# Position block 2 of a convolution in two fp32r parts, norm sums on ScalarE, skip weights in the block matrix

## The chip, the cores and the metric

The kernel runs on one core of a Trainium2 chip. The metric is the time of one execution on the device in microseconds, median of several runs. All 27 inputs lie in the chip's memory, and the output goes there.

## What is computed

Two layers, each of a mixing step and a feed-forward step, on x of 16 x 256 x 512 in fp32. The change is in the first mixing step, a long convolution:

```python
x = x + _L0_xattn_ref(_layernorm(x, axis=-1), L0_xattn_k, fside_S2_0, ctx_2048, ctx_2048, 8)

def _L0_xattn_ref(v, k, bias, x1, x2, num_heads):
    B, D, L = v.shape                        # 16, 256, 512
    H = D // num_heads                       # 32
    vr, x1r, x2r = (t.reshape(B, H, num_heads, L) for t in (v, x1, x2))
    kv = vr[:, :, :, None, :] * x2r[:, :, None, :, :]
    y = causal convolution of kv with k[h] along L
    skip = bias.reshape(H, num_heads)[None, :, :, None, None]
    y = y + kv * skip
    out = jnp.einsum('bhijl,bhil->bhjl', y, x1r)
    return out.reshape(B, D, L)
```

A layernorm follows at once (its rows feed the router of a mixture of eight experts), then that feed-forward step, an attention and a second feed-forward step. These are not touched.

## The kernel before, in words

Every engine has a queue of its own, in the order in which the Python code of a phase emits instructions (`p.do`, `p.dma`). Waits are semaphores: each `p.do` gets the tokens it waits for as its last arguments, and names its own result in the tables `T` and `U`. Nothing reorders the queues. An instruction that waits holds all that stands behind it on its engine.

The front phase (`front_phase`) does the convolution for 32 heads h. A head is 128 rows (16 batches x 8 channels) of 512 positions. The convolution is a Toeplitz product: positions are cut in four blocks of 128, and output block lb sums position blocks mb = 0 to lb, each a 128 x 128 matrix of filter values times a 128 x 512 matrix of products. The 512 columns are half of the (batch, i, j) triples, so each head is done in two halves, u = 0 and 1.

The steps of a head, with the lines of the code before:

- `load`: x, ctx in two layouts and the filter, by SyncE's queue, two heads ahead.
- `stats`, `shift`, `norm`: layernorm of the input rows. `stats` calls `layernorm_stats` (L115): bn_stats (L117), bn_aggr (L118) and an addition (L119) on VectorE, then a power of -1/2 on GpSimd (L120). `shift` (L315) is one product on VectorE, `norm` (L319) one ScalarE operation, which gives xn.
- `weigh` (L324) on VectorE: w = xn * skip * ctx. `skips`: a fp32 matmul of w with the block matrix ones_b (L338), and a product with ctx (L340), which gives sk. `residual` (L345) on GpSimd adds x.
- `filt`, `filt_lo`: the Toeplitz matrices. TensorE reverses them into PSUM tile PT (L301, L309), and ScalarE copies the high part th (L302) and the low part tl (L310). PT is one tile, so L309 waits for L302. `t0` (L311) on GpSimd is th + tl, in fp32.
- `turn`: TensorE transposes xn into PSUM tile PV (L331), ScalarE copies it (vt, L333).
- `product` (L354), GpSimd: kf, the products of a position block, five steps ahead of its use.
- `parts`, `lows`: kh (L361, ScalarE) is kf rounded to fp32r, kl (L369) the rest, on VectorE for block 0 and on GpSimd for block 1. Blocks 2 and 3 have no parts.
- `conv`: matmuls into PSUM tiles Y0 to Y3. Position blocks 0 and 1 take three fp32r matmuls (L386: th kh, tl kh, th kl), blocks 2 and 3 one fp32 matmul each (L381: t0 kf), which the trace shows as two records. VectorE multiplies Y with ctx (z, L393) and reduces over i (R, L399).
- `finish` (L404, L406) for the head before: R is transposed back, and out2 (VectorE) adds sk to it. That is x after the step. `stats0`, `shift0` (L475), `norm0` (L479), `turn0` (L486, L488) and `logit` (L493, L495) are its layernorm and the router's logits; `best` (L504, L505) picks two experts. turn, turn0 and logit share the PSUM tile PV.

The main loop writes all this out for u = 0 and 1 and lb = 0 to 3, eight steps per head. What stands in a step decides the queues' order. Of the loop's placement rules, these matter here:

```python
                if u == 1 and lb == 2 and h + 2 < n_heads:
                    stats(h + 2)
                if u == 0 and lb == 3 and more:
                    turn(h + 1)
                n = (2 * h + u) * 4 + lb + 4
                if n + 1 < len(units):
                    product(*units[n + 1])
                if n < len(units):
                    parts(*units[n], low=False)
                conv(h, u, lb, units[n] if n < len(units) and lb == 0 else None)
                if u == 0 and lb == 3 and h:
                    finish(h - 1)
                if h and u == 1:
                    (stats0, shift0, norm0, turn0)[lb](h - 1)
```

In the first eight heads, a shared weight of the next step is also split in the step u = 0, lb = 1 (L463 on ScalarE, L464 on GpSimd).

Of the kernel before, what the change touches and what calls it, by code (L numbers as in the profile page):

```python
# [123 lines left out]
def front_phase(nc, ctx, d, before, xa, idx, gat, n_heads=NHC):  # L124
# [88 lines left out]
    pad = m.sb("pad", [128, 3688])  # L213
# [187 lines left out]
    def finish(h):  # L401
# [4 lines left out]
        T["out2", h] = U["PR",] = p.do("vector", lambda e: e.tensor_tensor(xt[:, h % 4, :], sk[:, s, :], PR[:, :], ALU.add), g("pr", h), g("sk", h))  # L406
# [293 lines left out]
    load(1)  # L700
    stats(0)
# [17 lines left out]
    for h in range(n_heads):  # L719
        more = h + 1 < n_heads  # L720
        for u in range(2):
            for lb in range(4):
                if u == 0 and lb == 2 and h + 2 < n_heads:
                    load(h + 2)
                    clear(3)
                if u == 1 and lb == 2 and h + 2 < n_heads:
                    stats(h + 2)
# [17 lines left out]
                conv(h, u, lb, units[n] if n < len(units) and lb == 0 else None)  # L745
# [1008 lines left out]
```

How the kernel before makes its waits and increments, by code:

```python
    def emit(self, e, eng):  # L69
        seen = {}
        def wait(sem, v):
            if seen.get(id(sem), 0) < v:
                eng.wait_ge(sem, v)
                seen[id(sem)] = v
        for sem, v in self.before:
            wait(sem, v)
        for fn, waits, inc in self.q[e]:
            for w in waits:
                if w is not None:
                    wait(*w)
            ins = fn(eng)
            if inc:
                ins.then_inc(*inc)
# [1647 lines left out]
                def run(eng, e=e):  # L1733
                    for p in phases:
                        p.emit(e, eng)
                    if e == "sync":
                        for sem, v in before:
                            eng.wait_ge(sem, v)
```

## Time and profile before

| | before |
|---|---|
| median of 3 runs | 3311.36 us (3310.96 to 3315.59) |
| profiled execution, its own time | 3308.17 us |
| its span | 3306.4 us |
| TensorE busy (matmuls) | 3190.9 us, 97% |
| VectorE busy | 2164.9 us, 65% |
| ScalarE busy | 1269.4 us, 38% |
| GpSimd busy | 1014.3 us, 31% |
| L354, kf on GpSimd | 256 of 1179 ns |
| L393 and L399, z and reduce on VectorE | 256 each, of 680 and 684 ns |

The profile is of one execution. Times in it are microseconds from the start of the span. PE is TensorE, PEld its weight loads, DVE VectorE, ACT ScalarE, POOL GpSimd, SP SyncE. L393 is line 393 of the kernel. The ends of matmuls are modelled, so what a matmul costs is read from where the next one starts. The convolution ends at about 640 us, and TensorE shows as busy in nearly all of it. The shares of the whole span say little of it, since the last four fifths are other stages.

### The profile page before, as it was taken

How to read it: one execution, taken by the hardware profiler on the slowest of the kernel's cores; microseconds unless marked ns; L12 is line 12 of the kernel's file. 1: busy time of each engine (PE TensorE's matmuls, PEld its weight loads, DVE VectorE, ACT ScalarE, POOL GpSimd, SP SyncE). 2: the span in 40 equal slices, each digit the busy share in tenths (PEclk: the TensorE clock that was granted, in tenths of full speed). 3: DMA queues.
4: the chain of work that ended last, by engine and by line, in shares of the span. 5: the costliest groups of instructions: out<-in, count | busy, mean ns of one | idle time of the engine just before them, and what ended most of it. 6: DMA issues, size and time to landing. Idle time of an engine off the chain costs nothing.

```text
span 3306.4 us, 51716 instructions
## 1 busy us (share of the span) xinstructions
PE 3190.9 (97%) x18613; PEld 2698.1 (82%) x18613; DVE 2164.9 (65%) x5818; ACT 1269.4 (38%) x3059; POOL 1014.3 (31%) x1085
## 2 busy tenths in 40 slices
PE   7999999999999699999999999999997999999999
PEld 4666666688899579999999999999996777777777
DVE  6888888756555477888777778878876433322232
ACT  2333333233444255555555555555554311111111
POOL 6877777535111222222222222222201000000000
PEclk9999999999999899999999999999998999999999
DMA  4544443269544421111111111111101200000000
GB/s 131 156 139 131 135 136 90 79 201 311 180 153 153 177 93 53 46 46 46 46 46 46 46 46 46 46 46 44 34 14 55 81 26 26 26 26 26 26 13 13
DMA packets 123664, 267.21 MB, mean 81 GB/s; under 512 B 17668, under 2 KB 18316, under 8 KB 123414
## 3 DMA queue, kind: packets, MB, share of 16 engines
q1 hardware_dynamic: 100022, 186.40, 17.9%
q0 software_dynamic: 23392, 77.51, 7.1%
q8 instruction: 153, 2.51, 0.3%
q14 instruction: 97, 0.79, 0.1%
HBM read 159.29 MB, written 104.56 MB: 80 GB/s over the span
## 4 chain that ended last, share of the span: by engine, by line
PE 79%; DVE 10%; POOL 7%; ACT 1%; DMA 1%; issue 1%; SPq 0%; POOLq 0%; DVEq 0%; ACTq 0%
PE g_PH L1051 11%; PE g_O L1079 11%; PE t_U L1515 10%; PE t_S L1467 9%; PE t_PO L1502 5%; PE t_M L1451 5%; POOL c_kf L354 3%; PE t_T L1489 3%; PE f_Y L916 3%; PE f_Y L687 2%; PE f_Y L386 2%; PE t_M L1406 2%; PE f_Y L381 2%; DVE c_R L399 2%; DVE c_z L393 2%; PE t_M L1388 2%
## 5 line engine op out<-in xcount | busy, mean ns | idle before, releaser
L1477 ACT ACTIVATE t_pr<-t_sm,t_nb 128x256 f32<-128x256 f32 x512 | 256.5, 502 | 368.8 <-DVE t_nb L1473 368.8
L1064 DVE CAST g_hh<-g_hf 128x512 fp32r<-128x512 f32 x128 | 55.0, 429 | 481.8 <-PE g_O L1079 476.8
L1421 POOL TENSOR_TENSOR t_r<-t_r 128x256 f32<-128x256 f32 x128 | 96.0, 750 | 773.6 <-DVE t_rw L1483 457.6
L354 POOL TENSOR_TENSOR c_kf<-c_vt,c_ct 128x512 f32<-128x512 f32 x256 | 296.7, 1179 | 0.2 <-PE f_Y L381 0.2
L1063 ACT ACTIVATE g_hf<-g_PH,g_b1s 128x512 f32<-128x512 f32 x128 | 88.2, 689 | 536.9 <-PE g_PH L1051 536.9
L1484 DVE TENSOR_SCALAR t_pr<-t_pr,t_rw 128x256 f32<-128x256 f32 x512 | 223.5, 436 | 18.2
L386 PE MATMUL f_Y<-c_kh,c_th 128*128 128x512 f32 x448 | 200.9, 448 | 9.3 <-ACT c_kh L361 9.3
L1051 PE MATMUL g_PH<-g_xh,g_w1h 128*128 128x512 f32 x512 | 205.5, 401 | 1.5 <-DVE g_xl L1039 1.5
L1079 PE MATMUL g_O<-g_w2h,g_hh 128*128 128x512 f32 x512 | 205.2, 401 | 0.0
L1051 PE MATMUL g_PH<-g_xh,g_w1l 128*128 128x512 f32 x512 | 203.0, 397 | 0.0
L1051 PE MATMUL g_PH<-g_xl,g_w1h 128*128 128x512 f32 x512 | 203.0, 396 | 0.0
L1515 PE MATMUL t_U<-t_vol,t_oth 128*128 128x512 f32 x512 | 202.3, 395 | 0.0
L1515 PE MATMUL t_U<-t_voh,t_otl 128*128 128x512 f32 x512 | 202.0, 395 | 0.0
L1079 PE MATMUL g_O<-g_w2l,g_hh 128*128 128x512 f32 x512 | 201.7, 394 | 0.0
L1079 PE MATMUL g_O<-g_w2h,g_hl 128*128 128x512 f32 x512 | 201.5, 394 | 0.0
L1515 PE MATMUL t_U<-t_voh,t_oth 128*128 128x512 f32 x512 | 200.9, 392 | 0.0
L1473 DVE CUSTOM_DVE_ANT_0 t_sm<-t_S,t_mk 128x256 f32<-128x256 f32 x512 | 194.8, 418 | 7.7 <-PE t_S L1467 7.7
L393 DVE TENSOR_TENSOR c_z<-f_Y,c_ct 128x512 f32<-128x512 f32 x256 | 174.1, 680 | 35.7 <-PE f_Y L381 35.5
L1494 DVE TENSOR_TENSOR t_ptl<-t_T,t_pth 128x512 fp32r<-128x512 f32 x256 | 175.6, 686 | 15.5 <-ACT t_pth L1493 15.4
L381 PE MATMUL f_Y<-c_kf,c_t 128*128 128x512 f32 x384 | 185.4, 591 | 0.0
L399 DVE TENSOR_REDUCE c_R<-c_z 128x64 f32<-128x512 f32 x256 | 175.0, 684 | 6.7
L386 PE MATMUL f_Y<-c_kh,c_tl 128*128 128x512 f32 x448 | 178.1, 397 | 0.0
(361 smaller groups left out, 9666.5 us busy)
## 6 DMA issues: line engine op xcount, KB each, us to landing
xs<-c_zero SPq DMA_DIRECT2D x71, 256.0 KB, 5.2
f_xg<-xs SPq DMA_DIRECT2D x71, 256.0 KB, 2.8
ys<-f_yt POOLq DMA_DIRECT2D x71, 256.0 KB, 2.4
c_tr<-kpad SPq DMA_DIRECT2D x60, 256.0 KB, 4.6
f_xg<-xn SPq DMA_DIRECT2D x40, 256.0 KB, 4.4
c_xt<-x SPq DMA_DIRECT2D x32, 256.0 KB, 3.5
c_cr<-ctx SPq DMA_DIRECT2D x32, 256.0 KB, 3.8
c_ct<-ctxh SPq DMA_DIRECT2D x32, 256.0 KB, 4.3
```

Source lines behind the costliest of these rows:

```text
L354: T["kv", h] = T["kv1", n] = p.do("gpsimd", lambda e: e.tensor_tensor(o, iv, ic, ALU.mult), g("vt", h), g("ct", h), g("kl", n - 8), g("kh" ...
L381: last = p.do("tensor", lambda e, c=c, mb=mb: e.matmul(Y[y % 4][:, :], t0[:, s, c], kf[:, v, mb, :], start=False, stop=mb == lb), g("t0", ...
L386: last = p.do("tensor", lambda e, a=a, b_=b_, c=c, mb=mb, i=i: e.matmul(Y[y % 4][:, :], a[:, s, c], b_[:, v, mb, :], start=(mb == 0 and i ...
L393: T["z", h] = T["z1", y] = p.do("vector", lambda e: e.tensor_tensor(zz.rearrange("p (b j i) -> p b j i", i=8, j=8), iv, ic, ALU.mult), las ...
L399: T["red", y] = T["R", h] = p.do("vector", lambda e: e.tensor_reduce(rr, zr, AXX, ALU.add), g("z1", y), g("pr", h - 2))
L1051: T["ph", n] = p.do("tensor", lambda e, kk=kk, a=a, b_=b_, i=i: e.matmul(ph[:, :], a[:, k, kk, :], b_[:, s, kk, :], start=i == 0, stop=i = ...
L1079: tk = p.do("tensor", lambda e, a=a, b_=b_, t=t, fin=fin, c=c, beg=beg: e.matmul(O[t][:, :], a[:, n % 2, c], b_[:, k, :], start=beg, stop= ...
L1467: a = p.do("tensor", lambda e, t=t, j=j, q=q, k=k: e.matmul(PS1[:, 256 * t:256 * t + 256], q, k[:, s, :], start=j == 0, stop=j == 4), g("q ...
L1473: T["am", N] = am = p.do("vector", lambda e, t=t, k4=k4: e.tensor_tensor_reduce(out=sm[:, k4, :], in0=PS1[:, 256 * t:256 * t + 256], in1=m ...
L1477: T["ex", x] = p.do("scalar", lambda e, t=t, k4=k4: e.activation(pr[:, N % 2, t, :], sm[:, k4, :], ACT.Exp, bias=nb[:, k4, 0:1], scale=-1. ...
L1484: T["nm", x] = p.do("vector", lambda e, t=t, k4=k4: e.tensor_scalar(pr[:, N % 2, t, :], pr[:, N % 2, t, :], rw[:, k4, 1:2], None, ALU.mult ...
L1515: a = p.do("tensor", lambda e, t=t, tt=tt, j=j, o=o, w=w: e.matmul(PU[t][:, :], o[:, N % 3, tt], w[:, h, :], start=h == 0 and j == 0, stop ...
```

## The change

Three things are changed, all in the front phase.

Position block 2 is split in two fp32r parts as blocks 0 and 1 were: kh on ScalarE, kl on GpSimd for a half with u = 1 and on VectorE for one with u = 0. Its products are three fp32r matmuls in place of a fp32 one. Only block 3, which only meets filter block 0, stays fp32, so t0 shrinks to 128 columns.

The variances of both layernorms no longer come from bn_stats. For the input's norm, ScalarE sums the row (`total`), VectorE makes the negative mean, ScalarE sums the squares of the differences (`squares`). For the second norm, out2 becomes a tensor_tensor_reduce that also sums, then `squares0`. VectorE divides and adds epsilon, GpSimd takes the power as before. The shifts become products of two tiles.

The skip weight moves from w into the matrix of the skip product: ScalarE writes bs, ones_b times skip, per head, and w is a plain product.

```diff
-    kh = m.sb("kh", [128, 2, 2, 512], F32R)
-    kl = m.sb("kl", [128, 2, 2, 512], F32R)
-    t0 = m.sb("t0", [128, 2, 256])
+    kh = m.sb("kh", [128, 2, 3, 512], F32R)
+    kl = m.sb("kl", [128, 2, 3, 512], F32R)
+    t0 = m.sb("t0", [128, 2, 128])
...
+    def total(h):
+        s = h % 2
+        S_ = su[:, 0, s, :]
+        a = p.do("scalar", lambda e: e.activation(ju[:, :], xt[:, h % 4, :], ACT.Copy, accum_out=S_[:, 0:1]), g("x", h), g("xn", h - 2), U.get("ju"))
+        U["ju"] = a
+        T["mean", h] = p.do("vector", lambda e: e.tensor_scalar(S_[:, 1:2], S_[:, 0:1], -1.0 / 512.0, None, ALU.mult), a, g("xn", h - 2))
+
+    def squares(h):
...
+        T["sq", h] = U["ju"] = p.do("scalar", lambda e: e.activation(ju[:, :], xt[:, h % 4, :], ACT.Square, bias=S_[:, 1:2], accum_out=S_[:, 2:3]),
+                                    T["mean", h], g("x", h), U["ju"])
...
     def stats(h):
         s = h % 2
-        T["rs", h] = layernorm_stats(p, xt[:, h % 4, :], st[:, s, :], ag[:, s, :], rs[:, s, :], mhalf, g("x", h), g("xn", h - 2), c_mh)
+        S_ = su[:, 0, s, :]
+        a = p.do("vector", lambda e: e.tensor_scalar(S_[:, 3:4], S_[:, 2:3], 1.0 / 512.0, EPS, ALU.mult, ALU.add), T["sq", h], g("rs", h - 2))
+        T["rs", h] = p.do("gpsimd", lambda e: e.tensor_tensor(rs[:, s, :], S_[:, 3:4], mhalf, ALU.pow), a, c_mh, g("xn", h - 2))
...
     def shift(h):
         s = h % 2
-        T["nm", h] = p.do("vector", lambda e: e.tensor_scalar(nm[:, s, :], ag[:, s, 0:1], rs[:, s, :], -1.0, ALU.mult, ALU.mult), g("rs", h), g("xn", h - 2))
+        T["nm", h] = p.do("vector", lambda e: e.tensor_tensor(nm[:, s, :], su[:, 0, s, 1:2], rs[:, s, :], ALU.mult), g("rs", h), T["mean", h], g("xn", h - 2))
...
     def weigh(h):
         s = h % 2
-        T["w", h] = p.do("vector", lambda e: e.scalar_tensor_tensor(out=w[:, s, :], in0=xn[:, s, :], scalar=skip[:, h:h + 1],
-                                                                   in1=cr[:, s, :], op0=ALU.mult, op1=ALU.mult),
-                         g("xn", h), c_sk, g("cr", h), g("psk", h - 2))
+        T["bs", h] = p.do("scalar", lambda e: e.activation(bs[:, s, :], ones_b, ACT.Copy, scale=skip[:, h:h + 1]), c_ob, c_sk, g("psk", h - 2))
+        T["w", h] = p.do("vector", lambda e: e.tensor_tensor(w[:, s, :], xn[:, s, :], cr[:, s, :], ALU.mult), g("xn", h), g("cr", h), g("psk", h - 2))
...
-        if mb > 1:
+        if mb > 2:
             return
         T["kh", n] = p.do("scalar", lambda e: e.activation(kh[:, v, mb, :], kf[:, v, mb, :], ACT.Copy), g("kv1", n), g("mmu", 2 * h + u - 2))
-        if low or mb % 2:
+        if low or mb == 1 or mb == 2 and u:
             lows(h, u, mb)
...
-        eng = "gpsimd" if mb % 2 else "vector"
+        eng = "gpsimd" if mb == 1 or mb == 2 and u else "vector"
...
-        T["out2", h] = U["PR",] = p.do("vector", lambda e: e.tensor_tensor(xt[:, h % 4, :], sk[:, s, :], PR[:, :], ALU.add), g("pr", h), g("sk", h))
+        S_ = su[:, 1, s, :]
+        T["out2", h] = U["PR",] = p.do("vector", lambda e: e.tensor_tensor_reduce(
+            out=xt[:, h % 4, :], in0=PR[:, :], in1=sk[:, s, :], scale=1.0, scalar=0.0, op0=ALU.add, op1=ALU.add, accum_out=S_[:, 0:1]),
+            g("pr", h), g("sk", h), gu("xb", h - 2))
+        U["mean", h] = p.do("vector", lambda e: e.tensor_scalar(S_[:, 1:2], S_[:, 0:1], -1.0 / 512.0, None, ALU.mult), T["out2", h], gu("xb", h - 2))
+        squares0(h)
...
+                if u == 1 and lb == 0 and h + 2 < n_heads:
+                    total(h + 2)
+                if u == 1 and lb == 1 and h + 2 < n_heads:
+                    squares(h + 2)
                 if u == 1 and lb == 2 and h + 2 < n_heads:
                     stats(h + 2)
...
-                conv(h, u, lb, units[n] if n < len(units) and lb == 0 else None)
+                conv(h, u, lb, units[n] if n < len(units) and (lb == 0 or lb == 2 and not units[n][1]) else None)
```

`squares0`, `stats0` and `shift0` have the same form on the second half of su. In the new code the lines are: mean L423 and L295, squares0 L490, total L293, squares L300, the variances L496 (second norm) and L306 (input's norm), the shifts L501 and L329, kl L382, w L339, bs L338, turn's copy L346.

VectorE's queue, from out2 (head h - 1) to the input's variance of head h + 2. Before:

```order
L406 TENSOR_TENSOR c_xt<-c_sk,f_PR 128x512
L504 MAX c_mx<-c_lg 128x8
L505 MAX_INDEX c_ix<-c_mx,c_lg 128x8
L393 TENSOR_TENSOR c_z<-f_Y0,c_ct 128x512
L369 TENSOR_TENSOR c_kl<-c_kf,c_kh 128x512
L399 TENSOR_REDUCE c_R<-c_z 128x64
L117 BN_STATS c_st0<-c_xt 128x6
L118 BN_AGGR c_ag0<-c_st0 128x2
L119 TENSOR_SCALAR c_rs0<-c_ag0 128x1
```

Now:

```order
L420 ISA c_xt,c_su<-f_PR,c_sk 128x512
L420 ISA c_su 128x1
L423 TENSOR_SCALAR c_su<-c_su 128x1
L530 MAX c_mx<-c_lg 128x8
L531 MAX_INDEX c_ix<-c_mx,c_lg 128x8
L295 TENSOR_SCALAR c_su<-c_su 128x1
L406 TENSOR_TENSOR c_z<-f_Y0,c_ct 128x512
L382 TENSOR_TENSOR c_kl<-c_kf,c_kh 128x512
L412 TENSOR_REDUCE c_R<-c_z 128x64
L496 TENSOR_SCALAR c_su<-c_su 128x1
```

The mean of head h + 2 (L295), which needs ScalarE's `total`, stands ahead of z of block 0.

ScalarE's queue in the same place, from turn's copy vt to the second norm's xb. Before:

```order
L333 ACTIVATE c_vt<-f_PV 128x512
L302 ACTIVATE c_th<-f_PT 128x512
L361 ACTIVATE c_kh<-c_kf 128x512 x2
L310 ACTIVATE c_tl<-f_PT 128x512
L479 ACTIVATE c_xb<-c_xt,c_nm0,c_rs0 128x512
```

Now:

```order
L346 ACTIVATE c_vt<-f_PV 128x512
L490 ACTIVATE c_ju,c_su<-c_xt,c_su 128x512
L293 ACTIVATE c_ju,c_su<-c_xt 128x512
L316 ACTIVATE c_th<-f_PT 128x512
L374 ACTIVATE c_kh<-c_kf 128x512
L300 ACTIVATE c_ju,c_su<-c_xt,c_su 128x512
L374 ACTIVATE c_kh<-c_kf 128x512
L324 ACTIVATE c_tl<-f_PT 128x512
L374 ACTIVATE c_kh<-c_kf 128x512
L505 ACTIVATE c_xb<-c_xt,c_nm0,c_rs0 128x512
```

Squares of head h - 1 and total of head h + 2 stand ahead of th, squares of h + 2 between the kh of blocks 0 and 1, and the new kh of block 2 ahead of xb.

GpSimd's queue, a head in the later part (the products of three blocks in a row are one row with x3). Now:

```order
L367 TENSOR_TENSOR c_kf<-c_vt,c_ct 128x512 x3
L382 TENSOR_TENSOR c_kl<-c_kf,c_kh 128x512
L367 TENSOR_TENSOR c_kf<-c_vt,c_ct 128x512
L382 TENSOR_TENSOR c_kl<-c_kf,c_kh 128x512
L367 TENSOR_TENSOR c_kf<-c_vt,c_ct 128x512 x2
L497 TENSOR_TENSOR c_rs<-c_su,f_mhalf 128x1
L367 TENSOR_TENSOR c_kf<-c_vt,c_ct 128x512
L382 TENSOR_TENSOR c_kl<-c_kf,c_kh 128x512
L307 TENSOR_TENSOR c_rs<-c_su,f_mhalf 128x1
L325 TENSOR_TENSOR c_t<-c_th,c_tl 128x128
L367 TENSOR_TENSOR c_kf<-c_vt,c_ct 128x512
L358 TENSOR_TENSOR c_sk<-c_sk,c_xt 128x512
```

The second kl is new, the rest stands as before: the first power, kf, kl, the second power, t0, kf, sk.

## Rows read from the trace of the kernel before

**Rows 1.** Engines in one head: us, busy us and instructions, PE, PEld, DVE, ACT, POOL
```profile
284.50:303.50 19.00, 18.73 (x80) 12.97 (x79) 16.67 (x33) 6.28 (x11) 14.72 (x15) 1.00 0.46 139
```
**Rows 2.** Chain of waits through one head: start us, us, what
```profile
282.49 0.63 PE f_PV L331 x4
...
286.28 0.70 DVE c_z L393
...
287.69 0.59 DVE c_xt L406
...
288.64 0.59 DVE c_z L393
...
290.42 0.61 DVE c_st L117
...
291.27 0.15 DVE c_rs L119
...
298.06 2.51 POOL c_kf L354 x2
...
300.60 0.63 ACT c_kh L361
...
301.44 0.63 PE f_PV L331 x4
```
**Rows 3.** The same chain in two of the first eight heads, same instruction
```profile
123.29 2.51 POOL c_kf L354 x2
...
142.74 2.51 POOL c_kf L354 x2
```
**Rows 4.** Waits from 60 to 560 us: us in total, times, longest
```profile
PE f_PV L331 <- ACT c_lg L495: 13.2, 26, 1.2
```
**Rows 5.** Timeline of TensorE, convolution: start us, us, what
```profile
302.61 0.40 PE L386 MATMUL f_Y<-c_kh,c_th 128*128 128x512 f32 x1
302.85 0.40 PE L386 MATMUL f_Y<-c_kh,c_tl 128*128 128x512 f32 x1
...
303.32 1.88 PE L381 MATMUL f_Y<-c_kf,c_t 128*128 128x512 f32 x4
...
305.03 0.60 PE L404 MATMUL f_PR<-f_ident,c_R 128*128 128x128 f32 x4
```
**Rows 6.** ScalarE elsewhere: sums in the attention (timeline), a bias in a feed-forward (groups)
```profile
1603.70 0.51 ACT L1477 ACTIVATE t_pr<-t_sm,t_nb 128x256 f32<-128x256 f32 x1 [1.66 <-DVE t_nb L1473]
1604.12 0.19 ACT L1477 ACTIVATION_READ_ACCUMULATOR t_pr<-t_sm,t_nb 128x1 f32 x1
...
L1063 ACT ACTIVATE g_hf<-g_PH,g_b1s 128x512 f32<-128x512 f32 x128 | 88.2, 689 | 536.9 <-PE g_PH L1051 536.9
```
**Rows 7.** Timeline of VectorE in the attention: a tensor_tensor_reduce and its read-out
```profile
1603.25 0.41 DVE L1473 CUSTOM_DVE_ANT_0 t_sm<-t_S,t_mk 128x256 f32<-128x256 f32 x1
1603.59 0.07 DVE L1473 DVE_READ_ACCUMULATOR2_ANT t_nb<- 128x1 f32 x1
```
**Rows 8.** Timeline of GpSimd in the same head
```profile
291.50 0.55 POOL L120 TENSOR_TENSOR c_rs<-c_rs,f_mhalf 128x1 f32<-128x1 f32 x1 [4.06 <-DVE c_rs L119]
292.02 1.07 POOL L354 TENSOR_TENSOR c_kf<-c_vt,c_ct 128x512 f32<-128x512 f32 x1
293.04 1.28 POOL L369 TENSOR_TENSOR c_kl<-c_kf,c_kh 128x512 fp32r<-128x512 f32 x1
294.54 0.55 POOL L120 TENSOR_TENSOR c_rs<-c_rs,f_mhalf 128x1 f32<-128x1 f32 x1 [0.22 <-DVE c_rs L119]
295.06 0.73 POOL L311 TENSOR_TENSOR c_t<-c_th,c_tl 128x256 f32<-128x256 f32 x1
```
**Rows 9.** The instruction w (L324) and the kf beside it; min/median/max ns of w
```profile
L324 DVE SCALAR_TENSOR_TENSOR c_w<-c_xn,c_skip,c_cr x32: 750/1342/1462, 13.3 to 604.8; 128x512 f32<-128x512 f32 x32
...
297.27 1.34 DVE L324 SCALAR_TENSOR_TENSOR c_w<-c_xn,c_skip,c_cr 128x512 f32<-128x512 f32 x1
...
298.02 1.52 POOL L354 TENSOR_TENSOR c_kf<-c_vt,c_ct 128x512 f32<-128x512 f32 x1
```

More of the change, by code:

```diff
@@ L175, in front_phase @@
     w = m.sb("w", [128, 2, 512])
+    bs = m.sb("bs", [128, 2, 128])
     vt = m.sb("vt", [128, 2, 4, 128])
     kf = m.sb("kf", [128, 2, 4, 512])
-    kh = m.sb("kh", [128, 2, 2, 512], F32R)
-    kl = m.sb("kl", [128, 2, 2, 512], F32R)
-    t0 = m.sb("t0", [128, 2, 256])
+    kh = m.sb("kh", [128, 2, 3, 512], F32R)
+    kl = m.sb("kl", [128, 2, 3, 512], F32R)
+    t0 = m.sb("t0", [128, 2, 128])
     z = m.sb("z", [128, 3, 512])
@@ L185, in front_phase @@
     xb = m.sb("xb", [128, 2, 512])
+    ju = m.sb("ju", [128, 512])
+    su = m.sb("su", [128, 2, 2, 4])
     xT = m.sb("xT", [128, 4, 128])
-    st0 = m.sb("st0", [128, 2, 6])
-    ag0 = m.sb("ag0", [128, 2, 2])
     rs0 = m.sb("rs0", [128, 2, 1])
@@ L212, in front_phase @@
     rb = m.sb("rb", [8, 256])[:, :]
-    pad = m.sb("pad", [128, 3688])
+    pad = m.sb("pad", [128, 1168])
     sw = m.sb("sw", [128, 8192], F32R)
@@ L289, in split_filters @@
         T["kp",] = p.dma("gpsimd", ko, lambda e: e.dma_start(d["kpad"].rearrange("q h x -> h q x"), f32(kq[:, :, :])), a, b_)
+    def total(h):
[5 more added lines that the diff above has]
+    def squares(h):
+        s = h % 2
+        S_ = su[:, 0, s, :]
+        T["sq", h] = U["ju"] = p.do("scalar", lambda e: e.activation(ju[:, :], xt[:, h % 4, :], ACT.Square, bias=S_[:, 1:2], accum_out=S_[:, 2:3]),
+                                    T["mean", h], g("x", h), U["ju"])
     def stats(h):
         s = h % 2
-        T["rs", h] = layernorm_stats(p, xt[:, h % 4, :], st[:, s, :], ag[:, s, :], rs[:, s, :], mhalf, g("x", h), g("xn", h - 2), c_mh)
+        S_ = su[:, 0, s, :]
+        a = p.do("vector", lambda e: e.tensor_scalar(S_[:, 3:4], S_[:, 2:3], 1.0 / 512.0, EPS, ALU.mult, ALU.add), T["sq", h], g("rs", h - 2))
+        T["rs", h] = p.do("gpsimd", lambda e: e.tensor_tensor(rs[:, s, :], S_[:, 3:4], mhalf, ALU.pow), a, c_mh, g("xn", h - 2))
     def filt(h):
@@ L310, in filt_lo @@
             T["tl", h] = p.do("scalar", lambda e: e.activation(tl[:, s, :], PT[:, :], ACT.Copy), g("pt", h), g("mm", h - 2))
-        T["t0", h] = p.do("gpsimd", lambda e: e.tensor_tensor(t0[:, s, :], f32(th[:, s, 0:256]), f32(tl[:, s, 0:256]), ALU.add), g("th", h), g("tl", h), g("mm", h - 2))
+        T["t0", h] = p.do("gpsimd", lambda e: e.tensor_tensor(t0[:, s, :], f32(th[:, s, 0:128]), f32(tl[:, s, 0:128]), ALU.add), g("th", h), g("tl", h), g("mm", h - 2))
     def shift(h):
         s = h % 2
-        T["nm", h] = p.do("vector", lambda e: e.tensor_scalar(nm[:, s, :], ag[:, s, 0:1], rs[:, s, :], -1.0, ALU.mult, ALU.mult), g("rs", h), g("xn", h - 2))
+        T["nm", h] = p.do("vector", lambda e: e.tensor_tensor(nm[:, s, :], su[:, 0, s, 1:2], rs[:, s, :], ALU.mult), g("rs", h), T["mean", h], g("xn", h - 2))
     def norm(h):
@@ L337, in skips @@
         s = h % 2
-        T["psk", h] = p.do("tensor", lambda e: e.matmul(PSK[:, :], ones_b, w[:, s, :], start=True, stop=True),
-                           c_ob, g("w", h), g("sx", h - 1))
+        T["psk", h] = p.do("tensor", lambda e: e.matmul(PSK[:, :], bs[:, s, :], w[:, s, :], start=True, stop=True),
+                           g("bs", h), g("w", h), g("sx", h - 1))
         a = p.do("vector", lambda e: e.tensor_tensor(sk[:, s, :], cr[:, s, :], PSK[:, :], ALU.mult), g("psk", h), g("out2", h - 2))
@@ L379, in conv @@
             c = slice(128 * (lb - mb), 128 * (lb - mb) + 128)
-            if mb > 1:
+            if mb > 2:
                 last = p.do("tensor", lambda e, c=c, mb=mb: e.matmul(Y[y % 4][:, :], t0[:, s, c], kf[:, v, mb, :], start=False, stop=mb == lb),
@@ L467, in shared_weights, with squares0 @@
             ahead.append((fetch(part[0]), *part[1:]))
+    def squares0(i):
+        s = i % 2
+        S_ = su[:, 1, s, :]
+        U["sq", i] = U["ju"] = p.do("scalar", lambda e: e.activation(ju[:, :], xt[:, i % 4, :], ACT.Square, bias=S_[:, 1:2], accum_out=S_[:, 2:3]),
+                                    U["mean", i], T["out2", i], U["ju"])
     def stats0(i):
         s = i % 2
-        U["rs", i] = layernorm_stats(p, xt[:, i % 4, :], st0[:, s, :], ag0[:, s, :], rs0[:, s, :], mhalf, T["out2", i], gu("xb", i - 2), c_mh)
+        S_ = su[:, 1, s, :]
+        a = p.do("vector", lambda e: e.tensor_scalar(S_[:, 3:4], S_[:, 2:3], 1.0 / 512.0, EPS, ALU.mult, ALU.add), U["sq", i], gu("rs", i - 2))
+        U["rs", i] = p.do("gpsimd", lambda e: e.tensor_tensor(rs0[:, s, :], S_[:, 3:4], mhalf, ALU.pow), a, gu("xb", i - 2), c_mh)
     def shift0(i):
         s = i % 2
-        U["nm", i] = p.do("vector", lambda e: e.tensor_scalar(nm0[:, s, :], ag0[:, s, 0:1], rs0[:, s, :], -1.0, ALU.mult, ALU.mult), U["rs", i], gu("xb", i - 2))
+        U["nm", i] = p.do("vector", lambda e: e.tensor_tensor(nm0[:, s, :], su[:, 1, s, 1:2], rs0[:, s, :], ALU.mult), U["rs", i], U["mean", i], gu("xb", i - 2))
     def norm0(i):
@@ L700, in front_phase @@
     load(1)
+    total(0)
+    squares(0)
     stats(0)
@@ L709, in front_phase @@
     residual(0)
+    total(1)
+    squares(1)
     stats(1)
```

2 lines of the change are left out of this document (removed).

## The prediction

> **What bounds the kernel now.** I read the whole-span page first (the front phase, with the convolution, is the first fifth of the span), then the stretch of one head, then the chain of waits through it, then the timelines of each engine. One head of the convolution takes 18.95 us: in that stretch TensorE is busy 18.7 us of 19.0, VectorE 16.7, GpSimd 14.7, ScalarE 6.3 [rows 1]. That looks like a TensorE bound, but the chain [rows 2] is not one of matmuls. It is a ring that closes once per head. TensorE turns xn (L331), runs block 3 of the convolution and hands over after 3.79 us (282.49 to 286.28). VectorE works through its list for 8.26 us (286.28 to 294.54), up to the variance that GpSimd's power waits for. GpSimd then runs its own list for 6.06 us (294.54 to 300.60), and ScalarE makes kh, copies the logits out of PV and lets TensorE turn the next head after 0.84 us. 3.79 + 8.26 + 6.06 + 0.84 = 18.95. TensorE waits only 13.2 us in 26 heads for that last step, 0.5 us a head [rows 4]; so its own work is 18.45 us a head. The first eight heads have a ring of 19.45 us [rows 3], since ScalarE splits a shared weight in it.
>
> So the ring, not an engine's busy time, has to be recalculated. I take t = 0 where VectorE starts z of block 3 (u = 0).
>
> **TensorE.** A fp32r matmul of 512 columns starts 0.24 us after the one before (302.61, 302.85), a fp32 one takes 0.855 us (two from 303.32 to 305.03) [rows 5]; three parts cost 0.70. A half head (u) has three fp32 products, of which the two with position block 2 are split (in output blocks 2 and 3): four times 0.155 a head, 0.62 us off 18.45, leaves 17.8 us. One of the four lies in the ring: 3.79 becomes 3.64.
>
> **VectorE up to the first variance.** Before: z, reduce and out2 end at t = 2.00 (287.69 + 0.59), z of block 0 starts at 2.36, z, kl and reduce take 1.78, and the BN pair is done so that L119 stands at 4.99 (291.27) [rows 2]. Now: out2 also sums. The nearest rows are the attention's tensor_tensor_reduce with PSUM as one source, 0.41 us for 256 columns with a start-to-start of 0.34 [rows 7], and half of out2's 0.68; so the sum costs the read-out of some 0.08 alone. The mean (L423) takes 0.15 and hand-overs 0.08: t = 2.31. Now ScalarE must square (L490) and then total the head after next (L293), in this order, and **VectorE's L295 stands ahead of z of block 0 and waits for both**. A bare 512-column copy takes 0.63 (L361 in [rows 2]), one with a bias 0.69 [rows 6]; the read-out of the accumulator starts 0.42 after a 0.51 instruction and takes 0.19 [rows 6], so adds 0.10. Each also waits for the other's end through ju. Squares: 0.75 + 0.11; total: 0.63 + 0.11 + 0.03. ScalarE is done at 3.94 and z of block 0 starts at 4.05, 1.7 us later than before. ScalarE goes on with th (next start 0.54 later) and kh, which is done at 5.08: kl starts at 5.12, not 4.65. Reduce, then L496: 6.32, done 6.47. Removing bn_stats and bn_aggr (0.83 us, 290.42 to 291.27 less hand-over) is in this already: it gains 0.83, and the waits cost 1.7 + 0.5. GpSimd's first power starts at t = 6.54, where it started at 5.22 (291.50).
>
> **GpSimd.** Power 0.52, kf 1.02, kl 1.25, start to start [rows 8], must end before the second power: 6.54 + 2.79 = 9.33, where before it was free at 8.0 and waited for VectorE until 8.26. Then power, t0, kf, sk and two kf, 6.06 in all before. t0 has 128 columns for 256: 0.73 against kl's 1.28 for 512 gives 0.28 less.
>
> **The port.** w runs 0.75 us at the start, while GpSimd idles, and 1.34 in the median [rows 9]. One w starts at 297.27, beside sk, which ends where the kf behind it starts, at 298.02; w ends at 298.61, and that kf takes 1.52 for the usual 1.07 [rows 8, 9]. So sk finishes first, then w runs 0.6, and kf stands still for most of that. So, as I read it, a VectorE instruction with two tensors in SBUF and a GpSimd one exclude each other. By the Trainium skill (SBUF — State Buffer, Who interferes with whom) this is a lock held for a whole instruction, and a VectorE operation with two SBUF inputs takes part in it. The trace agrees, by 1.52 against 1.07 us. Another page speaks otherwise of w: the Trainium skill (Vector Engine (DVE) Microarchitecture Reference, Points that are easy to get wrong) has a scalar_tensor_tensor with two fp32 SBUF sources run at half rate; by it w would end some 0.6 us earlier, the kf in the ring might lose its 0.45 us of standing still, and the sum would be 13 us lower. The 0.75 us of the undisturbed w speaks against it; no run so far has the other form in its place.
>
> What this makes of the change: w as a plain product saves 0.07 at most (0.75 to 0.68) and still collides, so I count nothing; its copies of the weights (L338, a 128-column ScalarE operation of some 0.3 us) hide in ScalarE's idle time. No DMA is added or moved on any queue; the store of out2 starts 0.08 us later. The new kl of block 2 on VectorE (u = 0 of the next head) falls to t = 10.1, when GpSimd is in power and t0: it runs 0.60 between two GpSimd instructions and pushes t0 back by that, 0.60 in the ring. The shifts nm (L501, L329) are now products of two SBUF tensors of one column. Such a small one is not in the trace beside a busy GpSimd; bounds are nothing and the rest of the kl it meets. L501 comes up at t = 8.31, kl ends at 9.33: with the lock L306 ends at 9.61 and the second power starts at 9.68, without it at 9.35. I take the first, since the form is what the lock went by in [rows 9]. The other new kl (u = 1, GpSimd, 1.28 us) stands where GpSimd now idles 4.1 us before the first power [rows 8], so costs nothing, also with the 1.28 us that the shared weights add in eight heads; if the cover went, it would add 1.28. kh of block 2 hides in ScalarE, except where it stands between.
>
> **Sum.** 3.64 + 9.68 + (6.06 - 0.28 + 0.60 = 6.38) + 0.84 = 20.54 us with all port effects; 3.64 + 9.35 + 5.78 + 0.84 = 19.61 with none of the new ones. I take 20.4, nearer the first, +1.45 us a head. Twenty-nine heads (1 to 29) have both powers and a next turn: +42 us. The prologue gains 0.5 (ScalarE sums head 1 before it splits the filters), the first and last heads give back about 1 (their matmuls, 0.62 each). The profiled execution took 3308.2 us (span 3306.4), so its like would take about 3350; the median of the runs is 3311.4, 3.2 above, and goes to **3353**. A measurement of this kernel tells 0.2% (6.6 us) from no change.
>
> A second ring would hold the kernel even if GpSimd's were short. filt_lo on TensorE needs PT, which th frees. th now stands behind squares and total, and ends at t = 3.94 + 0.6; TensorE would reach filt_lo at t = 3.4 and from there has 10.85 us of work to the next turn. 3.64 + 4.54 + 10.85 = 19.0. So the matmul time saved in block 2 is lost here at the least.
>
> **Rivals.**
> - *TensorE becomes the bound, faster.* If ScalarE's two sums were there when VectorE has picked the best (0.36 us after the mean), the list to the second power would lose its two BN groups (0.83 each) and gain three small ones: some 7.1 us, and the ring 3.64 + 7.3 + 5.8 (6.4) + 0.84 = 17.6 to 18.2. Then TensorE's 17.8 decides: about 1.05 x 30 = 32 us less, 3279. For it: VectorE's busy time does fall. Against it: ScalarE starts only after out2 and the two sums take 1.6 us. It decides only if the wait at L295 is under 0.2 us; I have 1.3. 11%, with all weaker gains.
> - *The ring through PT alone, no change.* GpSimd gets ahead, and 19.0 us stands against 18.95: 3312. It needs the first power about 1.3 us earlier than I have it. 7%.
> - *No new port effect.* 19.6 to 20.0 us a head: 0.65 to 1.05 x 29 gives 3330 to 3342. For it: one-column operations may not take part. 13%.
> - *Accumulating costs full extra passes.* If out2's sum took 1.34, as w looks, +0.66 more a head, 21.1 us: 3374. Against it the 0.41 of rows 7. 7%.
> - *The forecast*, 20.1 to 20.8 us, 3344 to 3366: 62%.
>
> **How the numbers follow.** The range from 3322 to 3368 holds the forecast and the third rival, and leaves out the first, most of the second, and the fourth; about 8 in 10. Slower by over 0.2%: 62 + 13 + 7 = 82%; within: 7%; faster: 11%.
>
> **What would show it.** Right: a period of 20.4 us between turns; VectorE idle over 1 us ahead of z of block 0, put down to ScalarE's sum; the first power over 1 us later after z of block 3; TensorE waiting for c_lg by more than 1 us a head and for th at filt_lo; GpSimd without a gap between its kl and the second power; nm at 1 us where it was 0.2. Wrong, if the period is under 19 us, or if TensorE waits nowhere: then ScalarE's sums are shorter than a copy plus a read-out, or VectorE has enough else to do. That the fp32r parts are not cheaper would show as a block 2 over 2.2 us from its first matmul to its last start.

## The result and the profile after

The changed kernel takes 3343.16 us (median of 4 runs, 3342.24 to 3344.13); the kernel before, beside it on the same chip, takes 3311.16 us. The ratio is 1.0097 with a 95% interval from 1.0084 to 1.0109: 32 us slower, where 42 us were forecast. The profiled execution took 3342.2 us, its span 3340.5.

The chain of waits through one head, the same stretch as in [rows 2] (columns: start us, us, what):

```profile
295.48 0.63 PE f_PV L344 x4
...
299.09 0.70 DVE c_z L406
...
300.50 0.60 DVE c_xt L420
...
301.33 0.82 ACT c_ju L490 x2
...
302.24 0.72 ACT c_ju L293 x2
...
303.34 0.63 ACT c_kh L374
...
304.00 0.69 DVE c_kl L382
...
307.17 1.11 DVE c_nm L501
...
308.43 0.55 POOL c_rs L307
308.98 0.88 POOL c_t L325
...
314.67 0.63 ACT c_kh L374
...
315.51 0.63 PE f_PV L344 x4
```

It is still a ring of one head, now of 315.51 - 295.48 = 20.03 us, 1.08 more than before. Its pieces are TensorE's 3.61 (295.48 to 299.09), VectorE's 9.34 (to the second power at 308.43), GpSimd's 6.24 (to 314.67) and the turn's 0.84. New in it are two pairs of ScalarE, the squares and the total, between out2 and kl: each is a sum and its read-out. The same chain in two of the early heads:

```profile
110.31 0.63 PE f_PV L344 x4
...
130.85 0.63 PE f_PV L344 x4
```

These are 20.54 us apart, for 19.45 in [rows 3]. Twenty-nine heads by 1.08 are 31.3 us. The last reduction of the convolution starts at 672.2 us (L412), where it started at 642.5 (L399): 29.7 us later, which fits the ring less the 1.5 us that the prediction has the first and last heads give back. The two spans are 34.1 us apart; the 4 us behind the convolution, in stages that weren't touched, are not explained by any run.

VectorE's timeline around its two waits (start us, us, engine, line, operation, out<-in, shapes, in brackets the idle time before it and what ended it):

```profile
302.99 0.15 DVE L295 TENSOR_SCALAR c_su<-c_su 128x1 f32<-128x1 f32 x1 [1.35 <-ACT c_ju L293]
...
304.00 0.69 DVE L382 TENSOR_TENSOR c_kl<-c_kf,c_kh 128x512 fp32r<-128x512 f32 x1 [0.26 <-ACT c_kh L374]
...
307.17 1.11 DVE L501 TENSOR_TENSOR c_nm<-c_su,c_rs 128x1 f32<-128x1 f32 x1
308.21 0.14 DVE L306 TENSOR_SCALAR c_su<-c_su 128x1 f32<-128x1 f32 x1
...
308.87 0.68 DVE L382 TENSOR_TENSOR c_kl<-c_kf,c_kh 128x512 fp32r<-128x512 f32 x1
...
310.06 0.84 DVE L329 TENSOR_TENSOR c_nm<-c_su,c_rs 128x1 f32<-128x1 f32 x1
```

GpSimd's timeline over the same time:

```profile
305.43 0.55 POOL L497 TENSOR_TENSOR c_rs<-c_su,f_mhalf 128x1 f32<-128x1 f32 x1 [3.78 <-DVE c_su L496]
...
306.97 1.30 POOL L382 TENSOR_TENSOR c_kl<-c_kf,c_kh 128x512 fp32r<-128x512 f32 x1
308.43 0.55 POOL L307 TENSOR_TENSOR c_rs<-c_su,f_mhalf 128x1 f32<-128x1 f32 x1 [0.16 <-DVE c_su L306]
308.94 0.91 POOL L325 TENSOR_TENSOR c_t<-c_th,c_tl 128x128 f32<-128x128 f32 x1
```

VectorE stands idle for 1.35 us at L295, where it waits for ScalarE's total. Its shift of one column (L501) takes 1.11 us: it starts at 307.17 and ends at 308.28, as GpSimd's kl does (306.97 + 1.30 = 308.27). The second variance (L306) is queued behind it, and GpSimd's second power waits for that (0.16 us). Then the new kl of block 2 on VectorE (308.87) and GpSimd's t0 meet; t0 has half the columns it had and takes 0.91 us, where the whole one took 0.73 [rows 8] and the half one takes 0.46 in e4 below, with no kl beside it.

ScalarE's timeline shows the two sums, each an instruction and its read-out:

```profile
301.33 0.72 ACT L490 ACTIVATE c_ju<-c_xt,c_su 128x512 f32<-128x512 f32 x1 [4.10 <-DVE c_su L423]
301.96 0.19 ACT L490 ACTIVATION_READ_ACCUMULATOR c_ju<-c_xt,c_su 128x1 f32 x1
302.24 0.63 ACT L293 ACTIVATE c_ju<-c_xt 128x512 f32<-128x512 f32 x1
302.77 0.19 ACT L293 ACTIVATION_READ_ACCUMULATOR c_ju<-c_xt 128x1 f32 x1
```

The waits from 60 to 560 us, as in [rows 4] (us in total, times, longest):

```profile
PE f_PT L323 <- ACT c_th L316: 20.4, 24, 0.9
PE f_PV L344 <- ACT c_lg L521: 17.9, 23, 1.2
PE f_PV L512 <- ACT c_xb L505: 11.5, 25, 2.3
```

TensorE waits 0.85 us a head for th, 0.78 for the turn and 0.46 for xb, 2.1 in all, so that its own work is 17.9 us. The fp32r parts save about what they should (0.55 of 18.45, where 0.62 was forecast); TensorE waits for three things now instead of one, and the saving goes into these waits.

### The profile page after: what moved, and what is told of

It is laid out like the page before. It is cut to its first block, busy times and chain, and to the rows that moved or that the text cites. A ratio compares the mean times of both kernels' runs of the same rounds, so it can differ in the third digit from the quotient of the medians.

```text
span 3340.5 us, 52458 instructions
## 1 busy us (share of the span) xinstructions
PE 3182.0 (95%) x18741; PEld 2717.8 (81%) x18741; DVE 2185.8 (65%) x5818; ACT 1382.3 (41%) x3347; POOL 1060.8 (32%) x1117
## 4 chain that ended last, share of the span: by engine, by line
PE 78%; DVE 9%; POOL 7%; ACT 4%; issue 2%; DMA 1%; SPq 0%; POOLq 0%; ACTq 0%; DVEq 0%
PE g_PH L1085 11%; PE g_O L1113 11%; PE t_U L1549 10%; PE t_S L1501 9%; PE t_PO L1536 5%; PE t_M L1485 4%; POOL c_kf L367 3%; PE t_T L1523 3%; PE f_Y L950 3%; PE f_Y L713 2%; PE f_Y L399 2%; PE t_M L1440 2%; DVE c_R L412 2%; PE f_PSK L925 2%; PE t_M L1422 2%
## 5 line engine op out<-in xcount | busy, mean ns | idle before, releaser
L399 PE MATMUL f_Y<-c_kh,c_th 128*128 128x512 f32 x576 | 236.6, 411 | 9.2 <-ACT c_kh L374 9.2
L399 PE MATMUL f_Y<-c_kl,c_th 128*128 128x512 f32 x576 | 228.1, 396 | 0.0
L399 PE MATMUL f_Y<-c_kh,c_tl 128*128 128x512 f32 x576 | 227.4, 395 | 0.0
L1527 ACT ACTIVATE t_pth<-t_T 128x512 fp32r<-128x512 f32 x256 | 151.6, 592 | 67.2 <-PE t_T L1523 66.3
```

The costliest lines, as they stand in the source:

```text
L399: last = p.do("tensor", lambda e, a=a, b_=b_, c=c, mb=mb, i=i: e.matmul(Y[y % 4][:, :], a[:, s, c], b_[:, v, mb, :], start=(mb == 0 and i ...
```

## The experiments

In every one the time was taken in five rounds beside the kernel before. The kernel before took 3310.61 us beside the first four experiments, 3310.44 beside the next four (e5 to e8, on another chip) and 3308.59 beside the last three.

### One part of the change at a time

**e1_split: the split of block 2 alone.** To the kernel before is added only this part of the change, here its two main places:

```
-        if mb > 1:
+        if mb > 2:
             return
...
-        if low or mb % 2:
+        if low or mb == 1 or mb == 2 and u:
             lows(h, u, mb)
...
```

with t0 on 128 columns, and BN statistics and w as they were.

> The kernel before with the split of position block 2 alone (bn_stats and w as before). By the ring: TensorE's step 3.79 to 3.64, t0 0.28 shorter, and the new kl on VectorE falls between the second power and t0 and holds t0 back by 0.5 to 0.6; 18.95 becomes 19.0 us a head, so 3311 to 3318 us. Rival: TensorE's time decides, 0.62 us less a head, 3292 us. A kl that did not exclude GpSimd's work would give 18.5 us a head, 3297 us.

3315.52 us (3313.53 to 3324.64), ratio 1.0019 (1.0009 to 1.0029). The profiled execution is the slowest of the nine, and its span is 16.5 us longer; but its last reduction of the convolution starts only 5.8 us later than before (648.3 for 642.5 us). The rest lies behind the convolution, in stages that the split doesn't touch. In the later heads the ring is 18.97 us, nearly as before, but from other pieces: TensorE 3.62, VectorE 8.27, GpSimd 6.24, 0.84. What TensorE wins in the ring, t0 loses against VectorE's kl; its chain shows it (start us, us, what):

```profile
319.64 0.55 POOL c_rs L120
320.19 0.89 POOL c_t L311
```

In the early heads, though, no turn of TensorE is in the chain; it runs from GpSimd to VectorE and back, with the shared weight's residual (L464, 1.30 us at 133.39), a kf, the new kl (L369) and the kf that VectorE's next kl needs, in a row:

```profile
124.51 0.55 POOL c_rs L120
...
135.71 1.25 POOL c_kl L369
...
144.29 0.55 POOL c_rs L120
```

That ring is 144.29 - 124.51 = 19.78 us, 0.33 over the 19.45 of before [rows 3]: there the new kl on GpSimd has lost its cover.

**e2_skip: the skip weights alone.**

```
-        T["w", h] = p.do("vector", lambda e: e.scalar_tensor_tensor(... scalar=skip[:, h:h + 1], ...
+        T["bs", h] = p.do("scalar", lambda e: e.activation(bs[:, s, :], ones_b, ACT.Copy, scale=skip[:, h:h + 1]), ...
+        T["w", h] = p.do("vector", lambda e: e.tensor_tensor(w[:, s, :], xn[:, s, :], cr[:, s, :], ALU.mult), ...
```

> The kernel before with the skip weights in the block matrix alone; w is a plain product. By the reading that w takes 0.7 us in either form and the rest is waiting for GpSimd: w's median stays over 1.2 us, the ring stays at 18.9 to 19.0, 3311 us (3308 to 3313). Rival (the old form runs at half rate): w takes 0.7, kf is not held back, 18.5 us a head, 3298 us.

3309.94 us, ratio 0.9999 (0.999 to 1.0008): nothing, and the ring stays at 18.95. All w of this kernel, min/median/max ns:

```profile
L326 DVE TENSOR_TENSOR c_w<-c_xn,c_cr x32: 691/1346/1469, 13.8 to 604.8; 128x512 f32<-128x512 f32 x32
```

The plain product takes 1346 ns in the median, the form before took 1342 [rows 9]. Only the undisturbed one differs, 691 against 750 ns. The form of the instruction was never what made w long; GpSimd beside it is.

**e3_stats: the norm statistics alone**, all of the change but the other two parts.

> The changed kernel with blocks and skip weights as before, so only the norm statistics are changed. By the ring: VectorE's step is 9.34 as in the changed kernel, the others 3.79, 6.06 and 0.84: 20.0 us a head, 3343 us (3338 to 3348). Rival (the loss comes from the new kl and the copies of the split): under 3320 us.

3340.75 us (3337.37 to 3342.9), ratio 1.009 (1.0075 to 1.0106), 30 of the 32 us, with a ring of 19.99 us (294.75 to 314.74 in its chain). The shift of the second norm is as long as in the changed kernel. The other one is not (VectorE, then GpSimd, as in the timelines above):

```profile
306.60 1.09 DVE L501 TENSOR_TENSOR c_nm<-c_su,c_rs 128x1 f32<-128x1 f32 x1
...
308.99 0.15 DVE L328 TENSOR_TENSOR c_nm<-c_su,c_rs 128x1 f32<-128x1 f32 x1
```

```profile
308.36 0.72 POOL L324 TENSOR_TENSOR c_t<-c_th,c_tl 128x256 f32<-128x256 f32 x1
309.04 1.07 POOL L367 TENSOR_TENSOR c_kf<-c_vt,c_ct 128x512 f32<-128x512 f32 x1
```

It comes up at 308.99, as t0 ends (308.36 + 0.72) and 0.05 us ahead of the next kf, and takes 0.15 us; as I read it, it gets in between the two. In the changed kernel the same shift (L329, 310.06 to 310.90) comes up beside a kf (309.82 to 310.88) and ends with it, though sk follows on GpSimd at once (310.85). So such an instruction waits for the one GpSimd instruction that runs, not for GpSimd to be idle.

### One wait of the change at a time

**e4_ptr: the changed kernel with the two shifts in another form.** The same product, with the inverse deviation as the operand that holds one value per partition:

```
-... e.tensor_tensor(nm0[:, s, :], su[:, 1, s, 1:2], rs0[:, s, :], ALU.mult)
+... e.tensor_scalar(nm0[:, s, :], su[:, 1, s, 1:2], rs0[:, s, :], None, ALU.mult)
```

> The changed kernel with both shifts nm as tensor_scalar with a pointer operand, the form of before (one SBUF tensor as input in place of two). If the two-tensor form waits for GpSimd: nm takes 0.2 us in both places, the second power starts 0.1 to 0.2 us earlier (where kl ends), the period is 19.8 to 19.9, 3337 to 3340 us. If nm is long for another cause: nm stays at 1.1 and 0.84 us, 3343 us.

3334.6 us (3332.33 to 3336.03), ratio 1.0075 (1.0061 to 1.0088), 8.5 us under the changed kernel and a little better than expected; the shifts take about 0.2 us again. The ring is 19.80 us. It lost 0.23 and not the 0.9 by which L501 is shorter, because the second power has to wait for GpSimd's own kl in any case. It follows that kl at once now, where it stood 0.16 us behind it. VectorE's kl of block 2 comes up earlier too and holds back this power (0.95 us for 0.55) instead of t0, which takes 0.43 for 0.88; the two together take 1.38 us for 1.43. Chain of waits:

```profile
324.26 1.26 POOL c_kl L382
325.51 0.95 POOL c_rs L307
326.47 0.43 POOL c_t L325
```

**e5_early: the changed kernel with the total a step earlier**, so that its result is there when VectorE comes to L295:

```
-                if u == 1 and lb == 0 and h + 2 < n_heads:
+                if u == 0 and lb == 3 and h + 2 < n_heads:
                     total(h + 2)
```

> The changed kernel with the sum of head h + 2 (total and its mean) one step earlier, so that it no longer stands behind squares0 and ahead of th. By the ring: VectorE no longer waits at the mean; th and kh of block 0 end 0.76 us earlier, kl, reduce and the first power follow, 20.03 becomes 19.3 us a head, 3319 us (3316 to 3323). Rival (the wait at the mean is slack, kl or GpSimd decides): 3338 us or more.

3320.76 us (3316.68 to 3323.74), ratio 1.0031 (1.0019 to 1.0042), 22 us under the changed kernel, as expected. VectorE does L295 ahead of z of block 3 now, and only the squares, th and kh stand between out2 and kl:

```profile
289.59 0.14 DVE L295 TENSOR_SCALAR c_su<-c_su 128x1 f32<-128x1 f32 x1
...
294.46 0.69 DVE L382 TENSOR_TENSOR c_kl<-c_kf,c_kh 128x512 fp32r<-128x512 f32 x1 [0.94 <-ACT c_kh L374]
```

kl stands 4.09 us after z of block 3 (290.37), for 4.91 in the changed kernel; the ring is 19.21 us (the second powers start at 298.88 and 318.09). One statement in another place, with no operation changed, gives back two thirds of the loss.

**e6_early_ptr: both edits.**

> The one before and the shifts nm as tensor_scalar with a pointer, together. If the two add (0.76 and 0.23 a head): 19.0 to 19.1 us, 3311 to 3314 us, about the time of the kernel before. If TensorE's queue takes over through th and filt_lo: the same as the sum of head h + 2 alone, 3319 us.

3313.97 us (3308.35 to 3316.03), ratio 1.0007 (0.9998 to 1.0016), ring 19.00 us (313.95 to 294.95, second power). The two add up: 22 and 7 us. With them the change costs nothing measurable, but gains nothing either. It is still the same ring: TensorE's 3.61, VectorE's 5.52 from z of block 3 to the first power, GpSimd's 9.03 from there on, now without a wait for the second variance, and the turn's 0.84. VectorE still waits for kh in it, which stands behind the squares and th:

```profile
309.68 0.69 DVE L382 TENSOR_TENSOR c_kl<-c_kf,c_kh 128x512 fp32r<-128x512 f32 x1 [0.94 <-ACT c_kh L374]
```

### Another order, and a gain

In the ring GpSimd's second power can't start until VectorE has come to the input's variance, late in its list. Both powers could be asked for together, at the point of the first.

**e7_order: the kernel before, with both variances and powers behind kl of block 1.**

```
-                if u == 1 and lb == 2 and h + 2 < n_heads:
-                    stats(h + 2)
...
+                if u == 1 and lb == 1:
+                    if h:
+                        stats0(h - 1)
+                    if h + 2 < n_heads:
+                        stats(h + 2)
...
-                if h and u == 1:
+                if h and u == 1 and lb:
                     (stats0, shift0, norm0, turn0)[lb](h - 1)
```

> The kernel before with its arithmetic unchanged and only the order changed: both variances and powers stand together in the step u = 1, lb = 1, behind the kl of block 1 on GpSimd. By the ring: the second power starts 2.1 us earlier, the ring falls to about 16.8 us, and TensorE's own 18.45 us decide: 3296 us (3292 to 3300), TensorE without a wait at the turn. Rival (TensorE's matmuls already bound the kernel before, ring or not): 3308 to 3311 us.

3322.28 us (3317.05 to 3325.96), ratio 1.0035 (1.0024 to 1.0046), where 3296 was expected: a miss. The chain no longer passes GpSimd at all:

```profile
346.34 0.70 DVE c_z L393
...
349.29 1.26 DVE c_kl L369
...
355.07 0.14 DVE c_nm L475
...
355.23 0.82 ACT c_xb L479
...
356.09 0.65 PE f_PV L486 x4
...
365.58 0.70 DVE c_z L393
```

A second ring was overlooked. From z of block 3 VectorE's list to the second norm's shift (L475) is now 8.73 us long (7.06 before), with both BN groups in it and with a kl that takes 1.26 us beside GpSimd. ScalarE's xb comes 0.16 later and adds 0.86, and then TensorE, which waits for xb to turn the second norm, has 9.49 us before it until the next z of block 3: 19.24 us in all (346.34 to 365.58). What was taken off GpSimd's ring was put on this one.

**e8_best: the changed kernel, with the total at u = 0, lb = 3, the squares of h + 2, both variances and both powers behind kl of block 1, and the shifts as in e4.**

```
-                if u == 1 and lb == 0 and h + 2 < n_heads:
+                if u == 0 and lb == 3 and h + 2 < n_heads:
                     total(h + 2)
-                if u == 1 and lb == 1 and h + 2 < n_heads:
-                    squares(h + 2)
-                if u == 1 and lb == 2 and h + 2 < n_heads:
-                    stats(h + 2)
...
+                if u == 1 and lb == 1:
+                    if h + 2 < n_heads:
+                        squares(h + 2)
+                    if h:
+                        stats0(h - 1)
+                    if h + 2 < n_heads:
+                        stats(h + 2)
...
-                if h and u == 1:
+                if h and u == 1 and lb:
                     (stats0, shift0, norm0, turn0)[lb](h - 1)
```

> The changed kernel in that order: total of h + 2 one step earlier, squares of h + 2 behind kh of block 1, both variances and powers behind kl of block 1, nm with a pointer. By the ring: the first power at about 6.0, ring 17.9 to 18.2 us, TensorE's work 17.8: 18.0 to 18.2 us a head, 3283 to 3289 us, faster than the kernel before and than its reordered form, by the matmul time saved. Rival (ScalarE's sums or GpSimd's third kl hold it): over 18.45 us a head, 3296 us or more.

**3283.13 us** (3281.87 to 3288.97), ratio 0.9923 (0.9909 to 0.9936), faster than both kernels: 27 us under the one before, 60 under the change. The chain is TensorE's alone, head after head:

```profile
305.03 0.44 PE f_PV L344 x4
...
323.02 0.44 PE f_PV L344 x4
```

17.99 us a head, TensorE's own work. Here the order of e7 doesn't make the second ring long: the two variances are one-column instructions on VectorE (0.14 us each), so moving them forward lengthens its list by next to nothing.

**e9_order3: the kernel before, reordered without the new ring.** The input's statistics of h + 2 at u = 0, lb = 3, where VectorE idled before z of block 3, and the second norm's behind kl of block 1:

```
-                if u == 1 and lb == 2 and h + 2 < n_heads:
+                if u == 0 and lb == 3 and h + 2 < n_heads:
                     stats(h + 2)
...
+                if u == 1 and lb == 1 and h:
+                    stats0(h - 1)
...
-                if h and u == 1:
+                if h and u == 1 and lb:
                     (stats0, shift0, norm0, turn0)[lb](h - 1)
```

> The kernel before, arithmetic unchanged, other order: the input's variance of head h + 2 (bn_stats, bn_aggr, power) goes to the step u = 0, lb = 3, ahead of the z that VectorE waits for there, and the second norm's power behind the kl of block 1. If the reordered form before this lost by VectorE's longer list up to nm, xb and turn0 (a second ring): that list is now 7.1 us, as in the kernel before, or less, both rings are under 18.0 us, and TensorE's own 18.45 us decide: 3296 us (3292 to 3301). Rival (another cause, such as product waiting for matmuls): 3310 us or more again.

3293.11 us (3289.91 to 3298.17), ratio 0.996 (0.9947 to 0.9974), ring 18.48 us, TensorE's work of 18.45 as read from the kernel before. So 15 us were to be had without any of the change's arithmetic.

**e10_order3_split_skip: that order with the split and the skip part, BN statistics kept.**

> That order with the split and the skip part of the change, but with bn_stats. If the split's gain is TensorE's 0.62 us a head and appears once TensorE decides: 17.9 to 18.3 us a head, 3280 to 3292 us, so ScalarE's sums would not be needed. Rival (VectorE, at 17.3 us of work a head with the new kl, becomes the bound): 18.4 us or more, 3296 us or more, and the sums on ScalarE are what lets the split pay.

3319.51 us (3318.55 to 3321.29), ratio 1.0035 (1.0021 to 1.0049), ring 19.20 us. The rival's expectation came, not mine: with BN statistics and the kl of block 2, VectorE is the bound. Busy time from 400 to 480 us in e10, then in e8 (us, PE, PEld, DVE, ACT, POOL, each with its instructions):

```profile
400.00:480.00 80.00, 75.77 (x348) 57.57 (x347) 78.61 (x136) 33.17 (x62) 69.37 (x63) 1.00 0.47 141
```

```profile
400.00:480.00 80.00, 79.84 (x362) 60.23 (x361) 66.72 (x144) 41.80 (x91) 70.46 (x67) 1.00 0.45 134
```

In e10 VectorE is busy 78.6 us of 80. Its three kl a head take 1.18 to 1.50 us beside GpSimd, for an undisturbed length of 0.69; one of them:

```profile
410.81 1.49 DVE L369 TENSOR_TENSOR c_kl<-c_kf,c_kh 128x512 fp32r<-128x512 f32 x1
```

In e8 it has 13 us to spare and TensorE is full. So ScalarE's sums, the part that cost the change 30 us, are what lets the split pay in the right order. The two kernels also differ in where the statistics stand (e10 has e9's order, e8 its own); no run has the split with BN statistics in e8's order.

**e11_best_nosplit: e8 without the split.**

> The fastest form so far (sums on ScalarE, skip part, new order, nm with a pointer) with position blocks 2 and 3 in fp32 as before. TensorE's own 18.45 us decide: 3296 to 3300 us, 13 to 17 us over the form with the split. Rival (the ring still decides there, the split adds nothing): 3285 us or less.

3302.75 us (3299.43 to 3305.09), ratio 0.998 (0.9971 to 0.9989), ring 18.66 us (315.10 to 333.76) against 17.99 in e8. That is a little above what was expected: filt_lo (L323) takes 0.50 us in its chain, as in e8, and 0.23 in that of e9, since th now stands behind the squares. The 0.67 us is the price of the four fp32 products a head, put at 0.62. The split is worth some 20 us (3302.75 less 3283.13; 19 by the two ratios, since e8 ran on another chip) where TensorE decides, and nothing or less where it doesn't (e1).

## Why the prediction was right, and where its sizes were off

- **The ring.** Right: the kernel is a ring of one head over four engines and the change lengthens VectorE's step of it. Of the 32 us, 29.7 have built up by the end of the convolution: 29 heads by 1.08, less the ends, put at 1.5.
- **TensorE's step**, 3.64 forecast, measured 3.61, and its own work 17.8 forecast, 17.9 measured: right.
- **VectorE's step**, 9.68 forecast, measured 9.34: the main mis-sized term. The wait at L295 (over 1 us forecast, 1.35 measured) and z of block 0 (t = 4.05, measured 3.97) were right; kl came at 4.91 for 5.12, with 0.08 of it in that z and the rest in the hand-overs th, kh, kl, put too long; 0.2 us of the error are there. The rest is behind the stalled shift: the power follows the end of GpSimd's kl after 0.16 us, where 0.35 had been put. By e5 the total's place behind the squares was worth 22 us of the loss.
- **The port.** Right: the one-column shift takes part in it (1.11 us for 0.2), which the rival "no new port effect" denied; that rival is refuted by the row of L501 and by e4. Its price was less than the effect looks: 0.23 us a head by e4, where the sum had 0.33. By the Trainium skill (SBUF — State Buffer, Who interferes with whom) a VectorE instruction with two SBUF inputs contends with a GpSimd one that reads SBUF, and the page makes no exception for small ones. The traces agree down to one column, by 1.11 against 0.15 us.
- **GpSimd's step**, 6.38 forecast, measured 6.24: t0 was put at 0.42 and 0.60 more for the collision; with it, it takes 0.88. In e4, where no kl meets it, t0 takes 0.43, so the collision cost 0.45. VectorE's kl (308.87) starts before t0 does (308.94), so t0 waits for the rest of it only.
- **The value taken.** 20.4 us a head, nearer the full port effects; 20.03 came. The full sum of 20.54, less the 0.34 and 0.14 of the two steps, is 20.06. The 0.37 from 20.4 to 20.03, in 29 heads, are the 10 us by which the forecast was too high.
- **The new kl on GpSimd costs nothing**: right in the changed kernel, where GpSimd idles 3.78 us before the first power. Not right in general: in e1, where VectorE's next kl waits for the products behind it, it costs 0.33 us in each of the early heads.
- **The skip part at nothing**: right, by e2. The Trainium skill (Vector Engine (DVE) Microarchitecture Reference, Points that are easy to get wrong) has the old form of w run at half rate with two fp32 SBUF sources. The traces disagree: 750 ns undisturbed against 691 for the plain product, and no time gained by replacing it. The measurement decides.
- **The ring through PT.** TensorE does wait for th at filt_lo, 0.85 us a head, as foreseen. That this ring would hold the kernel at 19.0 if GpSimd's were short was not shown. The 19.00 of e6 are no sign of it: with the total moved th is done sooner, filt_lo starts at 309.18, 3.59 us after z of block 3, and TensorE waits at the turn instead, 1.0 us a head (26.2 us in 26 heads).
- **The signs.** Two came out smaller than announced: TensorE waits 0.78 us a head for the logits' copy (c_lg), not over 1, and GpSimd has a gap of 0.16 us between its kl and the second power, not none. The others came, the period as 20.03.
- **TensorE as the bound** was given 11% on the condition that VectorE waits under 0.2 us at L295. e5 and e6 remove that wait and e8's order was needed too before TensorE decided (17.99): the condition as I had put it was not enough.
- **Not foreseen in the experiments**: the ring through the shift, xb and TensorE's turn of the second norm, which undid e7. I had recalculated one ring, not looked for the next.

## What to carry to other kernels

Where no engine is full, find the ring and add up each engine's list between hand-overs; a part that shortens TensorE's work is worth nothing until the ring is shorter than that work (the split: nothing in e1, some 20 us between e11 and e8). When a reduction is moved to another engine, its result must not be waited for at the head of an in-order queue: ask for it a step earlier, which here was worth 22 us for one moved statement. And when the order is changed, recalculate every ring through the moved instruction, since what one loses another may gain.

## What the runs showed of the hardware

A VectorE product of two SBUF tensors waits for the GpSimd product that is running, down to one column: it took 1.11 us beside kl, for 0.15. It shows in the kernels above in a product of 8 columns too (f_gac, L522), in e7 beside a busy GpSimd and in the kernel before beside an idle one, VectorE's timelines:

```profile
370.98 1.20 DVE L522 TENSOR_TENSOR f_gac<-c_sm,f_gac 128x8 f32<-128x8 f32 x1
```

```profile
213.70 0.17 DVE L522 TENSOR_TENSOR f_gac<-c_sm,f_gac 128x8 f32<-128x8 f32 x1
```

The same product written with a per-partition operand takes 0.2 us beside a busy GpSimd (e4). And the wait is for one GpSimd instruction only: L329 in the changed kernel ends with the kf beside it (310.90 and 310.88), though sk follows, and in e3 one that is ready as t0 ends takes 0.15 us (at 308.99), though a kf follows.
